# Two score pairs of the first attention: the first pass of one head ahead of the other head's slot claim

## What is computed

```python
def _L0_attn_ref(x, w_kv_down, w_kv_up, w_q, w_out):      # x is layer-normed
    latent_kv = x @ w_kv_down
    kv = latent_kv @ w_kv_up
    k, v = (kv[..., :HD], kv[..., HD:])                   # 16 heads of 64
    q = (x @ w_q).reshape(Bx, Tx, N_HEAD, HEAD_SIZE)
    att = jnp.einsum('bqhd,bkhd->bhqk', q, k) * HEAD_SIZE ** (-0.5)
    att = jnp.where(causal, att, -jnp.inf)
    att = jax.nn.softmax(att, axis=-1)
    y = jnp.einsum('bhqk,bkhd->bqhd', att, v)
    return y.reshape(Bx, Tx, HD) @ w_out
```

## Time and profile before

| | |
|---|---|
| median of 3 runs | 2392.69 us (2391.76 to 2401.76) |
| the profiled execution, by its own time | 2397.04 us |
| its span in the trace | 2395.1 us |
| PE busy | 2188.9 us, 91% |
| DVE busy | 1677.2 us, 70% |
| ACT busy | 1379.9 us, 58% |
| mean granted TensorE clock | 0.968 of full speed |

### The profile page before, as it was taken

How to read it: one execution, slowest core, us unless ns; L and a number is a source line. 1 busy time by engine, 2 the same in 40 slices (tenths; PEclk the granted TensorE clock), 3 DMA queues, 4 the chain that set the end, 5 groups by cost and what they waited for, 6 DMA issues and landing times. The chain is left out here.

```text
span 2395.1 us, 49575 instructions
## 1 busy us (share of the span) xinstructions
PE 2188.9 (91%) x19395; PEld 1356.3 (57%) x19395; DVE 1677.2 (70%) x2042; ACT 1379.9 (58%) x2174; POOL 156.9 (7%) x283
## 2 busy tenths in 40 slices
PE   3699999999999999999999967999998998999998
PEld 2466666666666666766666744544444444444443
DVE  8677667676767676677767683677776776777781
ACT  4456565655556555656565643266665665666666
POOL 2101010000101010101010012010000000000000
PEclk8899999999999999999999987999999999999999
DMA  4000000000000000000000056011111111111000
GB/s 106 11 0 0 0 0 0 0 0 0 0 0 0 0 0 0 0 0 0 0 0 0 0 74 201 25 18 21 19 19 29 19 20 28 28 28 19 11 2 11
DMA packets 41093, 41.19 MB, mean 17 GB/s; under 512 B 21345, under 2 KB 33601, under 8 KB 40866
## 3 DMA queue, kind: packets, MB, share of 16 engines
q1 hardware_dynamic: 39458, 38.00, 8.0%
q10 hardware_dynamic: 1536, 1.69, 0.3%
HBM read 27.71 MB, written 11.70 MB: 16 GB/s over the span
## 5 line engine op out<-in xcount | busy, mean ns | idle before, releaser
L1543 DVE TENSOR_REDUCE nm_half<-slot 128x2 f32<-128x1024 f32 x512 | 607.5, 1222 | 202.5 <-PE slot L1305 149.8
L1526 ACT ACTIVATE pT<-slot 128x1024 f32<-128x1024 f32 x512 | 505.4, 1026 | 282.9 <-PE slot L1409 229.2
L810 ACT ACTIVATE prob<-slot,negmax 128x1024 f32<-128x1024 f32 (+6 forms) x448 | 316.5, 717 | 230.1 <-DVE negmax L857 153.9
L662 PE MATMUL slot<-k_hl,q_hl 64*128 64x512 f32 (+3 forms) x2560 | 359.9, 374 | 64.8 <-ACT prob L810 62.2
L662 PEld LDWEIGHTS slot<-k_hl,q_hl 64*128 64x128 f32 x2560 | 263.9, 198 | 107.1 <-ACT prob L810 40.1
L679 PEld LDWEIGHTS slot<-ident,prob 128*128 128x128 f32 x2304 | 254.1, 141 | 87.9 <-issue 61.9
L679 PE MATMUL slot<-ident,prob 128*128 128x128 f32 x2304 | 288.3, 275 | 0.0
L549 DVE COPY probT<-slot 128x768 f32<-128x768 f32 (+1 forms) x192 | 166.9, 869 | 162.7 <-PE slot L679 160.0
L691 PE MATMUL yspace<-probT,v_sb 128*64 128x512 f32 (+3 forms) x1536 | 275.9, 494 | 0.0
L1375 PE MATMUL yspace<-pT,v 128*32 128x512 f32 x2048 | 267.6, 604 | 1.6 <-ACT y_raw L1513 0.8
L1300 PE MATMUL slot<-ks,qs 48*128 48x512 f32 x1024 | 244.4, 475 | 21.2 <-issue 9.4
(11 more groups left out here) (235 smaller groups left out, 2539.2 us busy)
## 6 DMA issues: line engine op xcount, KB each, us to landing
qs<-q_hi SPq DMA_DIRECT2D x60, 64.0 KB
qs<-q_lo SPq DMA_DIRECT2D x60, 64.0 KB
ks<-k_hi SPq DMA_DIRECT2D x60, 64.0 KB
ks<-k_lo SPq DMA_DIRECT2D x60, 64.0 KB
x_tok<-in_L_attn_x_dram SPq DMA_DIRECT2D x4, 512.0 KB, 8.1
q_hi<-qk_out SPq DMA_DIRECT2D x4, 512.0 KB, 5.1
q_lo<-qk_out SPq DMA_DIRECT2D x4, 512.0 KB, 4.9
k_hi<-qk_out SPq DMA_DIRECT2D x4, 512.0 KB, 5.1
```

The costliest lines, as they stand in the source:

```text
L662: last = nc.tensor.matmul(own_ps[a][:, o:o + m], q_hl[hq][own, i * P:(i + 1) * P], k_hl[hk][own, o:o + m], start=(k == 0), stop=(k == 3 an ...
L810: last = nc.scalar.activation(prob[a][:, p_at(i, 0, w)], ps[:, o:o + w], ACT.Exp, bias=negmax[:, i, a:a + 1], accum_out=sums[:, i, a:a + 1])
L1526: nc.scalar.activation(pT[hp][m % PT_DEEP][:, :, :], slot[at["x", n] % RING][:, :].rearrange("p (j t) -> p j t", t=BANK), ACT.Exp)\
L1543: nc.vector.tensor_reduce(nm_half[:, h, :, p * TPB + i], slot[pos % RING][:, :].rearrange("p (a t) -> p a t", t=BANK), AX.X, ALU.max, nega ...
```

## The change

Two pairs, n = 5 and n = 7, are entered in a table `LONE` with the number 1. For them head 0's space is claimed, head 0's first pass is issued alone, then head 1's space is claimed, head 1's first pass is issued alone, and passes 1 to 3 follow with the heads side by side as before. All other score tiles keep their order; the passes are written as a helper. The masks and the signals come at the same place, after the last pass.

```diff
+                LONE = {5: 1, 7: 1}
...
+                            def one_pass(k, heads):
+                                hq, hk = ((0, 0), (0, 1), (1, 0), (1, 1))[k]
+                                for o in range(0, w, BANK):
+                                    m = min(BANK, w - o)
+                                    for a in heads:
+                                        own = slice(a * HS, (a + 1) * HS)
+                                        nc.tensor.matmul(own_ps[a][:, o:o + m], q_hl[hq][own, i * P:(i + 1) * P], k_hl[hk][own, o:o + m],
+                                                         start=(k == 0), stop=(k == 3 and o + m < w))
+                            passes = range(4)
                             if a0 is None:
...
+                            elif n in LONE:
+
+                                for a in range(2):
+                                    own_ps[a] = score_claim(n + a)[:, 0:w]
+                                    for k in range(LONE[n]):
+                                        one_pass(k, (a,))
+                                passes = range(LONE[n], 4)
                             else:
                                 own_ps = [score_claim(n + a)[:, 0:w] for a in range(2)]
-                            for k, (hq, hk) in enumerate(((0, 0), (0, 1), (1, 0), (1, 1))):
+                            for k in passes:
                                 if n == 0 and k == 2:
 
                                     freed(pe, it - 1, TQ)
-                                for o in range(0, w, BANK):
-                                    m = min(BANK, w - o)
-                                    for a in range(2):
-                                        own = slice(a * HS, (a + 1) * HS)
-                                        last = nc.tensor.matmul(own_ps[a][:, o:o + m], q_hl[hq][own, i * P:(i + 1) * P], k_hl[hk][own, o:o + m],
-                                                                start=(k == 0), stop=(k == 3 and o + m < w))
+                                one_pass(k, range(2))
```

More of the change, by code:

```diff
@@ L648, in scores @@
                                 freed(pe, it - 1, TK)
+                            own_ps = [None, None]
+                            def one_pass(k, heads):
[7 more added lines that the diff above has]
+                            passes = range(4)
                             if a0 is None:
```

## The result

| | before | after |
|---|---|---|
| median of 6 runs | 2396.95 us (2391.76 to 2401.76) | 2384.16 us (2383.19 to 2385.60) |
| profiled execution, own time | 2397.04 us | 2384.38 us |
| its span | 2395.1 us | 2382.4 us |
| mean granted clock | 0.968 | 0.976 |

The ratio is 0.9948, 95% interval 0.9931 to 0.9964: 0.5% faster. Three more runs of before, beside the runs of after, moved its median up by 4 us; the profiled executions, on which the sum was made, differ by 12.66 us.

What follows compares the result with a forecast made beforehand. TensorE, busy 91% of the span, was taken to bound the kernel, its clock falling in the first attention. 2397.04 - 16.1 (falls) + 8.6 (scores(7)) + 1.2 (one fall left) = 2390.7, say 2391 us; 80% range 2385 to 2402.

Steps and rivals of the forecast that it cites:

- 16.1 us of clock falls: First attention: TensorE's falls to half clock cost 16.1 us over 32 turns, 1.15 each; the change would end nearly all.
- two bounds: Clock in the first attention: either all falls gone (-16.1 us) or none gone (0); the first was taken.
- scores(5) gains nothing at full clock: scores(5): the lone pass fills 0.37 of 0.92 us of stall, but scores(5) ends where it did, 0 us gained.
- head 1's first matmul stands in the queue behind head 0's second, 0.34 later than before: scores(7): head 1 waits for head 0's 512- and 128-column matmuls, starts 0.34 us later, and its chain ends 0.29 later.
- 0.27 a turn and 8.6 us: scores(7): cost taken for its lone pass, 0.27 us a turn, 32 x 0.27 = 8.6 us.
- The lower bound of 0.14: scores(7): least cost a turn, 0.23 us for a 512-column step less 0.09 of slack before gates; 4.5 us in all.
- Rival 2: scores(7): cost mostly hidden by sharing with head 0's short second matmul and the wait before gates; 0.08 a turn, 2384.7 us; chance 0.09.
- slack before gates: After scores(7): a wait before gates would take up to 0.05 of the 0.29 us delay, 0.09 in the lower bound.
- the claim between the passes at 0.03: scores(7): the claim between the lone passes, a wait already met, may cost some 0.03 us.
- sign of error: Full-clock turn, forecast at 40.6 us: 40.4 us or less would show the forecast wrong and point to rival 2.
- one fall left, +1.2 us: First attention: one clock fall would remain in 32 turns, adding 1.2 us.
- Rival 1: First attention: the clock falls stay and the lone passes are a pure cost; 2401.6 us; chance 0.18.

Runs made afterwards that it cites:

- the first experiments: The experiments told first: the changed kernel with the lone pass kept only in scores(5), 2379.58 us, or only in scores(7), 2399.64 us.

## Why the prediction was wrong

**Right: what falls, and where.** The 16.1 us of clock falls were the term that decided, all of it came back, and work in the stall of scores(5) is what brought it: the thrown-away pass does it, the lone pass of scores(7) alone doesn't, and a matmul of 128 columns takes only some of them away (8 left, where 14 stood). But that one pass would be enough was picked between two bounds, not worked out: no row ahead of the run told how much work in the stall it takes, and with 128 columns the same choice would have been wrong.

**Right: scores(5) gains nothing at full clock, and scores(7) is put to the wrong head.** With scores(5) alone turns take 40.33; the cost of scores(7) vanishes when the head whose space is free goes first.

**Wrong: the step "head 1's first matmul stands in the queue behind head 0's second, 0.34 later than before".** It starts 0.11 after head 0's first, ahead of head 0's second. The step took the program's order for the order of the starts. Here matmuls on different rows of the array overtook one another, by three where eight stood ahead. From the step came 0.29, then 0.27 a turn and 8.6 us; measured are 0.08 a turn, 2.56 us. The lower bound of 0.14 stood on the same step and was too high as well. Rival 2 named this price to the hundredth (0.08, 2384.7 us), with a chance of 0.09, and that is luck, since its mechanism is not what happened: head 1 doesn't start behind head 0's short second matmul, and there is no slack before gates, which start 0.11 us after the last mask matmul before (473.26 - 473.15) and 0.12 after (510.41 - 510.29, the second of the two in the row at 510.22). The side term, the claim between the passes at 0.03, was the only real cost, at 0.08. The prediction had also named its sign of error: a full-clock turn of 40.4 us or less.

The rule cited from the Trainium skill ("TensorE: Matmul & The Clock Gate", Part 3, The mechanism), that matmuls start strictly in program order even on different rows, says the same as the failed step. The rows of scores(7) after show otherwise, 508.82 ahead of 509.05, and the measurement decides. The evidence ahead of the run could not tell: in the kernel before, the heads alternate, so program order and free rows give the same starts.

**Wrong in size: one fall left, +1.2 us.** None was left in the profiled execution of any kernel with a full pass of work in the stall of scores(5), except the two at 11.9 us where scores(7) was pulled apart. Together: 2390.7 - 6.1 - 1.2 = 2383.4, and 0.8 us more in the rest of the span gives 2384.2, against 2384.38 for the profiled execution. (One product in the prediction is rounded low: 32 x 0.35 is 11.2, not 11.1; nothing rests on it.)

**The chances.** Rival 1, the falls stay, is out. The range's lower end left half of rival 2 outside, and the result fell into that half; with a bound from 0 for the late start it would have begun at 2382 (2380.9 + 1.2). That the profiled execution stood above the median of the first three runs was taken for fewer falls in those; the median of six, 2396.95, is 0.1 us from the profiled one. The narrow spread after (2.4 us, against 10 before) fits a stage that no longer has falls. The falls of single runs were not counted, but their mean granted clocks are on record and go with the times: of the 13 runs of before beside the first experiments, the two fastest (2391.1 and 2391.2 us) had 0.970 and 0.971, the three slowest (2398.8 to 2400.5 us) 0.965 or 0.966.

**What beats the change.** scores(5) alone, with one lone pass (2379.58 us) or two (2377.68 us), or both pairs with both claims first in scores(7) (2380.29 us), are 0.6 to 0.7% under before. Their stages lie within 0.6 us of each other, so none of the three is shown to be the best.

## What to carry to other kernels

Two stalls of under a microsecond each were followed here by a fall of TensorE's clock in 14 turns of 32, at 1.15 us a fall, on top of their own length; look at the granted clock in the same place of every turn, not at its mean, and test with work that is thrown away before rearranging real work. Starting a unit's half early fills a stall only where that half's space is the first to come free: compare the two releases first. A met claim between two streams that share the array cost 0.08 us a turn here and nothing when it stood ahead of the first matmul, so put met claims there.

## What the runs showed of the hardware

Matmuls that use different rows of the array (0 to 63, 64 to 127) didn't keep the program's order of starts: with two, four and eight matmuls of head 0 standing ahead of it (scores(7) with one, two and four lone passes), head 1's first matmul started ahead of one, three and three of them, in all 32 turns. A claim of two met waits between two such streams delayed the second by 0.10 us (508.82 against 508.71; 0.01 with the claim ahead of both). One pass of one head per turn, put into the 0.92 us stall, went with a clock at 1.00 in 32 turns of 32, where 14 had fallen, also when its result was thrown away.
